# Expert 7's one-hot, gate and activation transposes inside the down projection of expert 6, and expert 7's down projection in other banks, by halves

## The reference

```python
def _expert(x, g, b, W1, b1, W2, b2, Wo, bo):
    x = _layernorm(x, g, b)
    x1 = x @ W1 + b1                                   # 1024 -> 512
    x2 = jnp.clip(x @ W2 + b2, -20.0, 20.0)
    hidden = jnp.clip(x1 * (x2 * jax.nn.sigmoid(x2)), -10000.0, 10000.0)
    return jnp.clip(hidden @ Wo + bo, -10000.0, 10000.0)   # 512 -> 1024
...
scores, idx = jax.lax.top_k(logits, K)                 # K = 2
gate = jax.nn.softmax(scores, axis=-1)
gates_e = jnp.zeros((N, E), xf.dtype).at[jnp.arange(N)[:, None], idx].add(gate)
...
    return (acc + gcol[:, None] * _expert(xf, g, b, w1, bb1, w2, bb2, wo, bbo), None)
...
x = x + _L0_gnn_ref(_layernorm(x, axis=-1), ...)
x = x + _L0_ffn_ref(_layernorm(x, axis=-1)[None], ...)[0]
```

## Time and profile before

| | us |
|---|---|
| median of 3 runs | 538.8 |
| lowest, highest run | 538.48, 543.7 |
| span of the profiled execution, first to last instruction | 537.0 |
| busy: PE, DVE, ACT, POOL | 496.9, 399.3, 283.2, 189.5 |
| mean granted TensorE clock, share of full speed | 0.970 |

### The profile page before, as it was taken

One profiled execution on the slowest core, in us unless ns is written; L12 is line 12 of the kernel. 1 busy time (PEld: TensorE's weight loads), 2 busy tenths in 40 slices (PEclk: granted clock), 3 DMA queues, 4 the chain that ended last, 5 costly groups with the idle time before them and its releaser, 6 DMA issues.

```text
span 537.0 us, 6836 instructions
## 1 busy us (share of the span) xinstructions
PE 496.9 (93%) x2583; PEld 439.1 (82%) x2583; DVE 399.3 (74%) x654; ACT 283.2 (53%) x406; POOL 189.5 (35%) x164
## 2 busy tenths in 40 slices
PE   3899999999999999999999999758999999999984
PEld 2899999999999987788888887646887877877772
DVE  5756989954444345589886875887898898898985
ACT  3443342423424225498886215436788688688630
POOL 5100443665564102288885822150020000000462
PEclk9999999999999999999999998759999999999988
DMA  8359566442334532302006362366869889888453
GB/s 303 134 213 385 120 264 239 158 158 89 147 94 150 194 105 78 131 1 79 1 1 234 125 237 99 136 241 233 320 249 422 342 340 414 344 304 361 162 191 119
DMA packets 21073, 106.33 MB, mean 198 GB/s; under 512 B 4864, under 2 KB 5248, under 8 KB 11312
## 3 DMA queue, kind: packets, MB, share of 16 engines
q1 hardware_dynamic: 15472, 91.53, 44.9%
q0 software_dynamic: 3696, 7.96, 4.5%
q10 hardware_dynamic: 1872, 6.39, 4.0%
HBM read 98.97 MB, written 6.91 MB: 197 GB/s over the span
## 4 chain that ended last, share of the span: by engine, by line
PE 56%; DVE 26%; ACT 9%; DMA 4%; issue 3%; POOL 1%; SPq 0%; ACTq 0%; DVEq 0%
PE ps L1156 51%; DVE lo L748 15%; ACT xg L665 3%; PE ps L1220 3%; ACT hi L569 3%; DMA raw<-in_wg 2%; DVE eqt L835 1%; ACT xg_hi L669 1%; DMA xg<-z_rows,slot_tok 1%; DVE x2sg L1069 1%; DMA z_rows<-xfb 1%; DVE small L753 1%; PE ps L1264 1%; ACT x2sg L674 1%; DVE ht_lo L1028 1%
## 5 line engine op out<-in xcount | busy, mean ns | idle before, releaser
L748 DVE TENSOR_TENSOR lo<-raw,hi 128x2048 fp32r<-128x2048 f32 x70 | 161.7, 2332 | 46.8 <-ACT hi L569 46.6
L569 ACT ACTIVATE hi<-raw 128x2048 fp32r<-128x2048 f32 x70 | 131.6, 1912 | 68.8 <-PE ps L1156 57.4
L454 POOL DMA_INDIRECT mask_rows<-colf,bits x48 | 61.8, 1287 | 93.7 <-DVE bits L843 44.2
L481 POOL TENSOR_SCALAR pr<-pr,small 128x384 f32<-128x384 f32 x48 | 59.1, 1249 | 53.5 <-DVE small L857 53.5
L1156 PE MATMUL ps<-xt_hi,hi 128*128 128x384 f32 x192 | 65.4, 341 | 2.2 <-DVE xt_lo L764 2.2
L1156 PE MATMUL ps<-xt_lo,hi 128*128 128x384 f32 x192 | 65.2, 339 | 0.0
L1156 PE MATMUL ps<-xt_hi,lo 128*128 128x384 f32 x192 | 65.1, 339 | 0.0
L1156 PE MATMUL ps<-hi,xg_hi 128*128 128x512 f32 x128 | 51.6, 403 | 5.7 <-DVE lo L748 3.9
L1156 PE MATMUL ps<-hi,xg_lo 128*128 128x512 f32 x128 | 50.9, 397 | 0.0
L1156 PE MATMUL ps<-lo,xg_hi 128*128 128x512 f32 x128 | 50.8, 397 | 0.0
L1156 PE MATMUL ps<-t_hi,hi 128*128 128x384 f32 x128 | 43.1, 337 | 0.6 <-DVE t_lo L794 0.6
(11 more groups left out here) (212 smaller groups left out, 1045.9 us busy)
## 6 DMA issues: line engine op xcount, KB each, us to landing
raw<-in_wf SPq DMA_DIRECT2D x42, 1024.0 KB, 7.0
raw<-in_wg SPq DMA_DIRECT2D x28, 1024.0 KB
xfb<-in_wf SPq DMA_DIRECT2D x6, 1024.0 KB, 7.4
src_i<-in_srcb ACTq DMA_DIRECT2D x4, 768.0 KB, 4.2
dst_i<-in_dstb ACTq DMA_DIRECT2D x4, 768.0 KB, 8.7
y_rows<-y SPq DMA_DIRECT2D x6, 512.0 KB, 3.0
xin<-in_x SPq DMA_DIRECT2D x3, 512.0 KB, 4.7
xres<-in_x SPq DMA_DIRECT2D x3, 512.0 KB, 4.1
```

The lines of the kernel that those rows point to most:

```text
L454: pool.indirect_dma_start(out=mbuf[:, :], out_offset=bass.IndirectOffsetOnAxis(ap=bits[:, 1, g:g + 1], axis=0), in_=colf[:, 5, g:g + 1], i ...
L481: pool.tensor_scalar(pr[:, h % 3, i, :], pr[:, h % 3, i, :], rinv[:, h % 3, i:i + 1], None, ALU.mult).then_inc(normalised, 1)
L569: act.activation(hi[SLOT[c]][:, :], raws[RAW[c]], ACT.Copy).then_inc(hi_done, 1)
L748: dve.tensor_tensor(lo[SLOT[c]][:, :], raws[RAW[c]], f32(hi[SLOT[c]][:, :]), ALU.subtract).then_inc(lo_done, 1)
```

## The change

PE does the slot work right after expert 7's x1, before the down projection of expert 6, and not after it. It does expert 7's `turn_hidden` between the two halves of that down projection. The down projection of expert 7 goes to banks 1 and 0 (`LAST_Y`) and no longer waits for `store_y(6)`; the sums that were in banks 0 and 1 go to banks 3 and 4. On DVE the copy of the gates comes right behind expert 7's hidden activations, `hidden_lo(7)` comes between the last two chunk splits, and the four `add_rows` are spread between the steps of expert 7's output, of which each half is clipped as soon as its chunk is used. The programs of ACT, POOL and SP are not edited.

```diff
--- before.py
+++ after.py
@@ -302,7 +302,8 @@
         y_lo = [lo[SLOT[c]][:, 0:D] for c in (UP_LAST, UP_LAST + 1)]
         slot_gate = r3[:, 7, 0:2]
         lg, eq, ranked, oh1, gates, oh2, pos, tmp, posm, over_gate = (r8[:, j, :, :] for j in range(10))
-        SUM_BANKS = [(0, 1), (5, 6), (2, 7)]
+        SUM_BANKS = [(3, 4), (5, 6), (2, 7)]
+        LAST_Y = [B[1], B[0]]
         LOGITS = [B[0][:, 0:NE], B[0][:, NE:2 * NE], B[3][:, 4 * NE:5 * NE]]
         TOK_BANK = [B[2], B[4]] + [B[7]] * (NE - 2)
 
@@ -1079,6 +1080,13 @@
                     dve.wait_ge(h_turned, e)
                 link(dve.tensor_tensor(hh[:, :], B[0], sg[:, :], ALU.mult))
                 dve.tensor_scalar(hh[:, :], hh[:, :], 10000.0, -10000.0, ALU.min, ALU.max).then_inc(h_ready, 1)
+                if e == NE - 1:
+                    dve.wait_ge(last_oh_turned, 1)
+                    dve.tensor_copy(slot_gate, B[7][:, 0:2]).then_inc(slot_gates, 1)
+                    split_lo(CHUNKS - 2)
+                    hidden_lo(NE - 1, (NE - 1) % 2)
+                    split_lo(CHUNKS - 1)
+                    break
                 for k in nxt[3:6]:
                     if k:
                         split_lo(k)
@@ -1094,29 +1102,35 @@
                 dve.scalar_tensor_tensor(out=y_lo[e][:, cut], in0=y[:, e, cut], scalar=slot_gate[:, e:e + 1], in1=f32(y_hi[e][:, cut]),
                                          op0=ALU.mult, op1=ALU.subtract).then_inc(y_lo_done, 1)
 
-            hidden_lo(NE - 1, (NE - 1) % 2)
+            halves = [slice(0, CW), slice(CW, D)]
+
+            def last_y(half):
+                dve.wait_ge(chunk_used, CHUNKS - 1 + half)
+                dve.tensor_scalar(y[:, 1, halves[half]], LAST_Y[half], 10000.0, -10000.0, ALU.min, ALU.max).then_inc(y_half, 1)
+
+            def last_add(half, t):
+                dve.wait_ge(last_summed, NT * half + t + 1)
+                if t == NT - 1:
+                    dve.wait_ge(tile_added, 1)
+                dve.tensor_tensor(xres[:, t, halves[half]], xres[:, t, halves[half]], B[SUM_BANKS[t][half]],
+                                  ALU.add).then_inc(out_ready, 1)
+
             store_y(NE - 2, (NE - 2) % 2)
-            dve.wait_ge(last_oh_turned, 1)
-            dve.tensor_copy(slot_gate, B[7][:, 0:2]).then_inc(slot_gates, 1)
-            for n in range(3):
-                add_rows(n)
+            add_rows(0)
             dve.wait_ge(y_hi_done, 1)
             y_rest(0, slice(0, D))
+            last_y(0)
+            add_rows(1)
+            dve.wait_ge(y_hi_done, 2)
+            y_rest(1, halves[0])
+            last_y(1)
+            add_rows(2)
+            dve.wait_ge(y_hi_done, 3)
+            y_rest(1, halves[1])
             add_rows(3)
-            dve.wait_ge(chunk_used, CHUNKS)
-            halves = [slice(0, CW), slice(CW, D)]
-            for half in range(2):
-                dve.tensor_scalar(y[:, 1, halves[half]], B[3 + half], 10000.0, -10000.0, ALU.min, ALU.max).then_inc(y_half, 1)
-            for half in range(2):
-                dve.wait_ge(y_hi_done, 2 + half)
-                y_rest(1, halves[half])
             for half in range(2):
                 for t in range(NT):
-                    dve.wait_ge(last_summed, NT * half + t + 1)
-                    if t == NT - 1:
-                        dve.wait_ge(tile_added, 1)
-                    dve.tensor_tensor(xres[:, t, halves[half]], xres[:, t, halves[half]], B[SUM_BANKS[t][half]],
-                                      ALU.add).then_inc(out_ready, 1)
+                    last_add(half, t)
             dve.wait_ge(out_ready, 2 * NT)
             with crowded(dve) as e:
                 dve.tensor_copy(fr[:, :, 7:8], over_gate[:, :, bass.ds(e, 1)])
@@ -1321,17 +1335,20 @@
                     ins.then_inc(chunk_used, 1)
 
             def down(e, par, c):
+                to = LAST_Y if e == NE - 1 else B[3:5]
                 pe.wait_ge(ht_lo_done, e + 1)
-                if e:
+                if e and e < NE - 1:
                     pe.wait_ge(y_ready, e)
                 for part in range(2):
                     cols = slice(D + part * CW, D + (part + 1) * CW)
-                    pe.matmul(B[3 + part], selx[:, e % 3, :], brow[:, cols], start=True, stop=False)
+                    pe.matmul(to[part], selx[:, e % 3, :], brow[:, cols], start=True, stop=False)
                 for part in range(2):
                     wait_lo(pe, c + part)
                     for k in range(HT):
-                        ins = three(B[3 + part], (ht_hi[:, par, k, :], ht_lo[:, par, k, :]), weight(c + part, k), False, k == HT - 1)
+                        ins = three(to[part], (ht_hi[:, par, k, :], ht_lo[:, par, k, :]), weight(c + part, k), False, k == HT - 1)
                     ins.then_inc(chunk_used, 1)
+                    if e == NE - 2 and part == 0:
+                        turn_hidden(NE - 1)
 
             def turn_hidden(e):
                 pe.wait_ge(h_ready, e + 1)
@@ -1340,6 +1357,18 @@
                 for k in range(HT):
                     ins = pe.transpose(B[2][:, k * P:(k + 1) * P], hh[:, k * P:(k + 1) * P], ident[:, :])
                 ins.then_inc(h_turned, 1)
+
+            def turn_slots():
+
+                pe.wait_ge(last_oh, 1)
+                pe.wait_ge(xg_scaled, 2 * NE)
+                for j in range(2):
+                    for t in range(NT):
+                        pe.transpose(B[5 + j][:, t * P:(t + 1) * P], last_rows[:, j, t, :], ident[:, :])
+                for j in range(2):
+                    for t in range(NT):
+                        ins = pe.matmul(B[7][:, j:j + 1], last_rows[:, j, t, :], gates[:, t, LAST[j]:LAST[j] + 1], start=t == 0, stop=t == NT - 1)
+                ins.then_inc(last_oh_turned, 1)
 
             turn_tokens(0, 0)
             pe.wait_ge(rows_ready, 1)
@@ -1355,19 +1384,12 @@
                 if e:
                     pe.wait_ge(h_ready, e)
                 up(B[0], e, par, c + 2, slice(0, CW))
+                if e == NE - 1:
+                    turn_slots()
                 if e:
                     down(e - 1, 1 - par, c + 4)
-                turn_hidden(e)
-
-            pe.wait_ge(last_oh, 1)
-            pe.wait_ge(xg_scaled, 2 * NE)
-            for j in range(2):
-                for t in range(NT):
-                    pe.transpose(B[5 + j][:, t * P:(t + 1) * P], last_rows[:, j, t, :], ident[:, :])
-            for j in range(2):
-                for t in range(NT):
-                    ins = pe.matmul(B[7][:, j:j + 1], last_rows[:, j, t, :], gates[:, t, LAST[j]:LAST[j] + 1], start=t == 0, stop=t == NT - 1)
-            ins.then_inc(last_oh_turned, 1)
+                if e < NE - 1:
+                    turn_hidden(e)
             down(NE - 1, 1, CHUNKS - 2)
 
             def add_last(j, halves, first):
```

## The result

| | before | after |
|---|---|---|
| median of 20 runs each, us | 538.97 | 545.36 |
| lowest, highest run, us | 537.81, 545.02 | 541.53, 548.87 |
| profiled execution: time, span, us | 538.8 (median), 537.0 | 545.88, 543.8 |
| its mean granted TensorE clock | 0.970 | 0.956 |

The ratio of the times is 1.008 with a 95% interval of 1.0052 to 1.0108, that is 2.8 to 5.8 us more: no change by the bound of 1% that the prediction used, but slower than before, since the interval leaves out 1. The runs of either kernel spread over 7 us, so the ratio says more than the two medians, and 1.008 of 538.97 is 543.3.

A forecast was written before the change was run, and what follows sets the result against it. PE's path to expert 7's down projection, with a 1.93 us wait and slow clock, was taken as the bound. Its 3.5 us gain is eaten and 3.0 us added: span 540.0, plus 1.8 around it, 541.8 us; range 538.0 to 543.8.

The forecast's parts named there:

- The 3.5 us: On PE, expert 7's down projection ends at 520.0, not 523.50: 1.93 us of wait saved, the rest slow clock.
- The wait that takes their place: DVE idles from 520.3 to about 525 for expert 7's `y_hi`, queued behind ACT's scalings, which await POOL's last gathers.
- The gathers: POOL's last three gathers wait for two-SBUF-input DVE instructions, ending at 515.6, 517.95, 519.35; the last two land 521.5, 522.9.
- the first rival: POOL's gathers not displaced: no hold-up by a split, or one slips in ahead of `add_rows(0)`; 540.6 us, chance 0.25.
- DVE against POOL: POOL's adds and DVE instructions with two SBUF inputs wait for each other; `add_rows(2)` waits until POOL ends at 527.95.
- The sum: At the end on DVE, the last six adds end at 534.8, not 531.76: gain eaten, 3.0 us added.
- The second rival: At the end, DVE's wait for ACT does not bind and POOL holds nothing up; -0.6, 538.2 us, chance 0.13.
- The third: Each POOL gather loses to one more DVE instruction, the last landing at 524.7; 543.2 us, chance 0.1.

The follow-up runs named there:

- `ht_lo(7)` last: Changed kernel with expert 7's `hidden_lo` behind both last chunk splits on DVE, as before the change; tail 39.56 us, ratio to before 1.0039.
- second execution: The unedited changed kernel profiled once more; tail 39.80 us against 40.36 in its first profile and 37.52 before; ratio to before 1.0065.
- ACT's order: Changed kernel with both halves of expert 7's `y_hi` ahead of the two scalings for POOL on ACT; tail 37.47 us, ratio to before 0.9997.
- DVE's order: Changed kernel with the four `add_rows` and two clips of expert 7 on DVE in the order of before; tail 37.72 us, ratio to before 1.0005.
- tile 2 gathered first: Changed kernel with the two gathers of tile 2 issued first of the six; tail 37.91 us, ratio to before 0.9991.
- adds on PE: Changed kernel with `y_hi` ahead of ACT's scalings, tile 2 summed last, POOL's two adds replaced by four PE identity matmuls; tail 35.20 us, ratio to before 0.9946.
- changed again: The changed kernel run once more without edits, beside the other versions; tail 39.80 us, ratio to before 1.0065 (1.0024 to 1.0106).
- the first experiment: Changed kernel with ACT making both halves of expert 7's `y_hi` before its two scalings for POOL; tail 37.47 us, ratio to before 0.9997.

## Why the prediction came out

**PE.** Right: the down projection ends at 519.94 (523.90 - 3.96), forecast 520.0, without idle time and at full clock. The 3.5 us are all there, and end in PE's wait of 2.89 us.

**The wait that takes their place.** Right in place and size. DVE is idle from 520.26 to 524.43 (3.96 taken off), forecast 520.3 to about 525, for `y_hi` behind ACT's scalings. That this order is the cause is shown by the two kernels that undo it on ACT or on DVE.

**The gathers.** Partly wrong, and this is the step that was mis-sized. The fourth gather was held up as forecast: it ends at 515.50, forecast 515.6, and the kernel with `ht_lo(7)` last shows the split to be what holds it. The fifth and sixth were not: they take 0.94 us each and end at 516.75 and 517.99, where I had 517.95 and 519.35. The fifth slipped in beside `add_rows(0)`, as the first rival had it; the two start within 0.1 us of each other (519.77 and 519.71). What I had against this, that a gather needs the memory only 0.1 us after its start (0.94 less 0.8), does not settle it: the third gather started 0.08 us into a split and was held, the fifth 0.06 us into `add_rows(0)` and was not (both in the last section). Yet the scalings begin at 521.40, forecast 521.5, since I took the time from an instruction's end to the landing as 3.6 us, and it was 519.77 + 5.50 - 520.71 = 4.56. Two errors cancelled, which is luck: 1.2 us of hold-up that did not come and 1.0 us of landing that did. The landing alone varies by 0.5 us between executions. A row of before could have warned me: its fifth gather, whose instruction also ended 1.25 us after the fourth's, landed up to 520.09 - 515.91 = 4.2 us after its end, and I had used the fourth and the sixth, whose instructions were longer. Why a short instruction lands later after its end is not shown. That transfers issued so close wait for each other was not tried; against it, the sixth gather of after lands 5.5 us after its start, as the fifth does, though it follows it by 1.24 us.

The Trainium skill, SBUF — State Buffer, section Who interferes with whom, infers that `tensor_tensor` doesn't hit descriptor generation. The 2.65 us against 1.90, for the same gather with the split's end moved, show that here it holds up the gather as a whole. The gather also reads its row numbers from SBUF, and whether this reading was held up or the making of descriptors, no run separates.

**DVE against POOL.** Right: `add_rows(2)` takes 2.79 (forecast: until POOL is done, which was 527.75 after 3.96, forecast 527.95), and without POOL's adds 1.28.

**The sum.** The last add ends at 534.53 after 3.96 are taken off, forecast 534.8: +2.8 us for +3.0, and +2.3 in the second execution. The second rival needed the wait not to bind and POOL to hold nothing up. ACT's order, DVE's order and tile 2 gathered first take away the wait, or most of it, but not the hold-up, and come to the tail of before, within 0.4 us; with both gone (adds on PE) the tail is 2.3 us shorter than before. The third needed a landing after 524 and did not occur.

**The rest.** The median of 545.36 lies above the forecast range, though 1.008 times the median of before, 543.3, is inside it. The 20 executions and the 12 of the row "changed again" both give a ratio 1.2 to 1.5 us above what the tail explains, within the intervals; the fastest executions (541.53 against 537.81, 541.02 against 537.99) are 3.0 to 3.7 us apart; the profiled execution shows 3.96 us of slow clock ahead of the edits. Whether the changed kernel meets these stretches more often than before, or by chance in these runs, stays open. No run separates it.

## What to carry to other kernels

When an engine on the chain of waits is made faster, ask which transfer or queue ends next, and follow it through each engine that runs in program order: here two scalings ahead of `y_hi` on ACT and two `add_rows` behind it on DVE turned one late landing into idle time of three engines. Work that nobody waits for yet belongs behind the step that others wait for. Where VectorE and GpSimd both add SBUF operands in the same microseconds, count the sum of their times and not the longer one; here the adds were better placed on PE, which stood idle.

## What the runs showed of the hardware

A gather that starts 0.4 to 1.2 us into a DVE instruction with two SBUF inputs ended 0.8 us after it (1.90 and 2.65 behind the splits, 1.38 at 520.44 with `add_rows(0)` from 519.74 to 521.01). Close to the instruction's beginning it can go either way. In the changed kernel the third gather started 0.08 us into a split and was held up to 0.82 us behind its end:

```profile
513.41 2.28 DVE L749 TENSOR_TENSOR lo<-raw,hi 128x2048 fp32r<-128x2048 f32 x1
```

```profile
513.49 3.02 POOL L504 DMA_INDIRECT yg<-y_rows,rows_u  x1 [0.30 <-issue]
```

The fifth started at 519.77, 0.06 us into `add_rows(0)`, and took its plain 0.94, while `add_rows(0)` took 1.32 instead of 1.28:

```profile
519.71 1.32 DVE L1098 SCALAR_TENSOR_TENSOR xres<-yg,r,xres 128x1024 f32<-128x1024 f32 x1
```

The second execution shows the same pair (3.02 at 0.07 us, 0.94 at 0.07 us). Why the split holds the gather at this distance and `add_rows` does not is open; I had expected the fifth to be held as well.

POOL's adds held up a DVE instruction with two SBUF inputs, but not one that took an input from PSUM: in the first experiment, with POOL adding from 523.48 to 529.16, the fourth `add_rows` took 3.46 us instead of 1.28, and the first two of the last adds 1.28 for both, their plain length.

The granted clock fell to 1.2 GHz for 7 us at 226 in one execution, behind a wait of PE of 0.84 us, and stayed at 2.4 GHz in another behind the same 0.84 us. The cause of the difference was not found.

An f32 matmul with the identity, 128x512, cost 0.9 us (3.60 for the four, at a granted clock of 1.00), against 0.23 for one of the split products.
